# High parts cast on ScalarE, block 0's weights copied on GpSimd, and the first clip ahead of the first additions

## What is computed

```python
d2 = q2[..., :, None] + k2[..., None, :] - 2.0 * qk
W = jnp.power(EPS + jnp.sqrt(jnp.maximum(d2, 0.0)), -2)
W = W / (EPS + jnp.sum(W, axis=-1, keepdims=True))
H = G * jnp.einsum('hbts,hbse->hbte', W, V)
```

## Time and profile before

| | before |
|---|---|
| median of three runs | 1596.91 us |
| the profiled execution | 1595.71 us |
| its span, first to last instruction | 1593.9 us |
| TensorE busy | 1420.5 us |
| VectorE busy | 1032.5 us |
| ScalarE busy | 928.3 us |
| GpSimd busy | 650.6 us |
| TensorE's mean granted clock | 0.962 |

### The profile page before, as it was taken

One profiled execution on the slowest core, in us unless ns is written; L12 is line 12 of the kernel. 1 busy time (PEld: TensorE's weight loads), 2 busy tenths in 40 slices (PEclk: granted clock), 3 DMA queues, 4 the chain that ended last, 5 costly groups with the idle time before them and its releaser, 6 DMA issues. The chain is left out here.

```text
span 1593.9 us, 23093 instructions
## 1 busy us (share of the span) xinstructions
PE 1420.5 (89%) x7425; PEld 902.2 (57%) x7426; DVE 1032.5 (65%) x1359; ACT 928.3 (58%) x646; POOL 650.6 (41%) x484
## 2 busy tenths in 40 slices
PE   6899999999999999999997568888983799999996
PEld 4555555555555555555454257777773566666664
DVE  7878988898889888988887635555566321221221
ACT  1779888988898889888989412222221122222221
POOL 5255456545654565456532612122120233333331
PEclk9999999999999999999999779999995899999998
DMA  4000000000000000000000312111120034233312
GB/s 144 14 1 14 27 26 13 13 26 26 13 13 26 26 13 13 26 27 13 7 13 14 112 57 97 39 52 40 46 81 13 21 85 138 33 84 84 87 28 71
DMA packets 67484, 66.91 MB, mean 42 GB/s; under 512 B 5152, under 2 KB 59936, under 8 KB 67424
## 3 DMA queue, kind: packets, MB, share of 16 engines
q1 hardware_dynamic: 60160, 56.58, 10.9%
q0 software_dynamic: 7296, 9.97, 3.7%
HBM read 48.70 MB, written 19.92 MB: 43 GB/s over the span
## 5 line engine op out<-in xcount | busy, mean ns | idle before, releaser
L1612 POOL TENSOR_TENSOR v_aug<-v_aug,wts 128x1024 f32<-128x1024 f32 x96 | 254.4, 2650 | 249.2 <-ACT wts L1465 244.6
L983 DVE TENSOR_SCALAR wts<-ps_s,k 128x1024 f32<-128x1024 f32 x240 | 297.1, 1279 | 86.3 <-PE ps_s L537 66.0
L1457 ACT ACTIVATE wts<-wts 128x4096 f32<-128x4096 f32 (+1 forms) x80 | 231.8, 2935 | 88.0 <-DVE wts L983 66.8
L552 PE MATMUL ps_o<-wts,g_r 128*64 128x512 f32 x1024 | 252.6, 616 | 12.7 <-ACT wts L1465 12.5
L1463 ACT ACTIVATE wts<-wts,eps_d 128x4096 f32<-128x4096 f32 (+1 forms) x80 | 241.6, 3019 | 0.2
L1465 ACT ACTIVATE wts<-wts 128x4096 f32<-128x4096 f32 (+1 forms) x80 | 235.2, 2940 | 2.5
L1378 DVE TENSOR_TENSOR wts<-rinv,ps_s 128x352 f32<-128x352 f32 x76 | 39.6, 521 | 254.5 <-ACT rinv L1530 171.3
L778 PE MATMUL ps_s<-wts,qk 128*128 x608 | 198.6, 470 | 3.2 <-issue 2.3
L972 DVE TENSOR_TENSOR v_aug<-v_aug,wts 128x1024 f32<-128x1024 f32 x96 | 156.1, 1626 | 5.4 <-ACT wts L1465 5.1
L537 PE MATMUL ps_s<-q_hi,k_hi 64*128 64x512 f32 x512 | 115.8, 446 | 41.2 <-DVE wts L983 31.1
L778 PEld LDWEIGHTS ps_s<-wts,qk 128*128 128x128 f32 x608 | 110.8, 192 | 65.2 <-issue 17.5
(11 more groups left out here) (238 smaller groups left out, 2411.7 us busy)
## 6 DMA issues: line engine op xcount, KB each, us to landing
wts<-in_w SPq DMA_DIRECT2D x16, 704.0 KB, 5.5
h_t<-o_raw SPq DMA_DIRECT2D x16, 512.0 KB, 2.7
qk<-h_t SPq DMA_DIRECT2D x16, 512.0 KB, 4.0
wts<-in_w SPq DMA_DIRECT2D x8, 640.0 KB, 7.1
raw_qk<-in_w_in SPq DMA_DIRECT2D x32, 128.0 KB, 2.2
raw_vg<-in_w_in SPq DMA_DIRECT2D x32, 128.0 KB, 2.2
acc<-wts SPq DMA_DIRECT2D x17, 128.0 KB, 1.8
wts<-in_x SPq DMA_DIRECT2D x2, 1024.0 KB, 5.9
```

The costliest lines, as they stand in the source:

```text
L552: mm = pe.matmul(ps_o[r, t], v_pair[:, b, r], wts[:, h, b, t], start=b == 0, stop=b == SB - 1)
L983: dve.tensor_scalar(wts[:, h, b, :], ps_s[:, h, :], k2[:, 2 * b + h:2 * b + h + 1], 0.0, ALU.add, ALU.max).then_inc(S_.max_ok, 1)
L1457: act.activation(chunk(start, end), chunk(start, end), ACT.Sqrt).then_inc(S_.sqrt_ok, 1)
L1612: pool.tensor_tensor(acc_w[:, 0], acc_w[:, 0], wts[:, 0, b], ALU.add).then_inc(S_.add_ok, 1)
```

## The change

It has four parts.

- The casts of q and k to their high parts move from VectorE's tail to ScalarE, between its square roots of blocks 6 and 7. They wait for q and k of the pair, and for the distances of the pair before, which still read the old high parts.
- A new semaphore, `acc0_ok`, and a new function `copy_first` on GpSimd, at the start of its body: it waits for block 0's weights and for the row sums of the pair before, and copies block 0 of both heads into `acc_w`, as a product with a column of ones.
- `add_first` then adds only block 1, into `acc_w` in place. `guard` of block 0 waits for the copies, that of block 1 for the additions, as before.
- On VectorE, `add_first` moves behind the guard of block 0 (in the last body, which has no guards, it stays where it was).

```diff
--- before.py
+++ after.py
@@ -247,7 +247,7 @@
         tok_i = sb("tok_i", [P, ET], U32)
         tok_now = sb("tok_now", [P, 2], U32)
 
-        names = ("x_in", "xb_in", "cst_in", "c_in", "fill_s", "fill_ok", "xnb_ok", "stats_ok", "aggr_ok", "std_ok", "rstd_ok", "xn_ok", "tr_ok", "xnt_ok",
+        names = ("x_in", "xb_in", "cst_in", "c_in", "fill_s", "fill_ok", "xnb_ok", "acc0_ok", "stats_ok", "aggr_ok", "std_ok", "rstd_ok", "xn_ok", "tr_ok", "xnt_ok",
                  "qk_in", "vg_in", "wqk_ok", "wvg_ok", "xh_ok", "x2_in", "q_proj", "k_proj", "v_proj", "g_proj", "norm_mm", "k2_mm",
                  "v_turned", "s_ready", "av_blk", "sum_mm", "q_ok", "k_cp", "vt_ok", "g_ok", "hi_ok", "split_ok", "qn1", "qn_ok", "k2_ok",
                  "v_ok", "max_ok", "h_ok", "sqq_ok", "sqk_ok", "add0_ok", "add_ok", "addb_ok", "gr_ok", "sqrt_ok", "ln_ok", "w_ok", "rln_ok", "r_ok", "h_out",
@@ -958,10 +958,9 @@
 
             def add_first(n):
                 dve.wait_ge(S_.w_ok, len(LOGS) * n + parts_until(LOGS, 1))
-                if not (isinstance(n, int) and n == 0):
-                    dve.wait_ge(S_.sum_mm, n)
                 for h in range(2):
-                    dve.tensor_tensor(acc_w[:, h], wts[:, h, 0], wts[:, h, 1], ALU.add).then_inc(S_.add0_ok, 1)
+                    dve.wait_ge(S_.acc0_ok, 2 * n + h + 1)
+                    dve.tensor_tensor(acc_w[:, h], acc_w[:, h], wts[:, h, 1], ALU.add).then_inc(S_.add0_ok, 1)
 
             def add_second(n, b):
                 dve.wait_ge(S_.w_ok, len(LOGS) * n + parts_until(LOGS, b))
@@ -972,8 +971,8 @@
                 dve.tensor_tensor(acc_w[:, 1], acc_w[:, 1], wts[:, 1, b], ALU.add).then_inc(S_.addb_ok, 1)
 
             def guard(n, b, free):
-                if not (isinstance(n, int) and n == 0) and b <= 1:
-                    dve.wait_ge(S_.add0_ok, 2 * n)
+                if b <= 1:
+                    dve.wait_ge((S_.acc0_ok, S_.add0_ok)[b], 2 * n)
                 if free is not None:
                     dve.wait_ge(S_.addb_ok, free)
                 dve.wait_ge(S_.s_ready, SB * (n - 1) + b + 1)
@@ -1023,8 +1022,8 @@
 
                 if ahead >= 1:
                     dve.wait_ge(S_.k2_ok, p + 2)
-                add_first(p)
                 if ahead == 0:
+                    add_first(p)
                     context()
                 for b in range(SB):
                     if b == 6 and not first:
@@ -1037,9 +1036,9 @@
                         add_second(p, b)
                     if ahead >= 1:
                         guard(p + 1, b, NA * p + (b - 1) if b >= 2 else None)
+                    if b == 0 and ahead >= 1:
+                        add_first(p)
                 copy_values(p)
-                if ahead == 2:
-                    split_high(p + 2)
                 if ahead >= 1:
                     copy_vt(p + 1, p + 3 if ahead == 2 else PAIRS)
                 if ahead == 2:
@@ -1448,9 +1447,18 @@
                 act.wait_ge(S_.rln_ok, n + 1)
                 act.activation(rinv[:], rinv[:], ACT.Exp, scale=-1.0).then_inc(S_.r_ok, 1)
 
-            def roots(n):
+            def split_high(n):
+                act.wait_ge(S_.q_ok, n + 1)
+                act.wait_ge(S_.s_ready, SB * (n - 1))
+                act.activation(q_hi[:], q32[:], ACT.Copy)
+                act.wait_ge(S_.k_cp, n + 1)
+                act.activation(k_hi[:], k32[:], ACT.Copy).then_inc(S_.hi_ok, 1)
+
+            def roots(n, ahead=False):
                 for start, end in ROOTS:
-                    if isinstance(n, int) and start in (2, 4):
+                    if ahead and end == SB:
+                        split_high(n + 1)
+                    if isinstance(n, int) and n == 0 and start in (2, 4):
                         turned_high(start + 2)
                         turned_high(start + 3)
                     act.wait_ge(S_.max_ok, NB * n + 2 * end)
@@ -1468,9 +1476,11 @@
 
             roots(0)
             weights(0, True)
-            with act.Fori(1, PAIRS) as p:
-                roots(p)
+            with act.Fori(1, PAIRS - 1) as p:
+                roots(p, ahead=True)
                 weights(p, False)
+            roots(PAIRS - 1)
+            weights(PAIRS - 1, False)
             rows(PAIRS - 1)
 
             def probs_t(i, k, n):
@@ -1603,6 +1613,13 @@
                     pool.wait_ge(S_.k2_mm, n)
                 pool.tensor_tensor(k_sq[:], k32[:], k32[:], ALU.mult).then_inc(S_.sqk_ok, 1)
 
+            def copy_first(n):
+                pool.wait_ge(S_.w_ok, len(LOGS) * n + parts_until(LOGS, 0))
+                if not (isinstance(n, int) and n == 0):
+                    pool.wait_ge(S_.sum_mm, n)
+                for h in range(2):
+                    pool.tensor_tensor(acc_w[:, h], wts[:, h, 0], unit, ALU.mult).then_inc(S_.acc0_ok, 1)
+
             def add_block(n, b):
                 pool.wait_ge(S_.w_ok, len(LOGS) * n + parts_until(LOGS, b))
                 if b == 2:
@@ -1619,6 +1636,7 @@
 
             def pair(p, first=False, ahead=2, later=3):
 
+                copy_first(p)
                 for b in range(2, SB):
                     if b == 4 and not first:
                         gate_rows(p - 1)
```

## The result

The changed kernel took 1658.45 us in the median of four runs (1657.16 to 1661.7), the kernel before 1596.62 in four: a ratio of 1.0392, with a 95% interval of 1.0374 to 1.041. The forecast was 1652 us.

The account below looks back on a forecast made before the run. Bound: a loop over the engines where ScalarE's weights and VectorE's tail meet at block 2's values, 53.0 us a pair. 14 x 4.1 = 57, less 1 for the last, 56; 1595.7 + 56 = 1652 us, range 1606 to 1662.

Parts of the forecast that it names:

- Step 1: ScalarE's hole before its last square root: the two moved casts, 2.1 us, fit with 0.3 us or more to spare.
- both strands: ScalarE's weights and VectorE's tail of copies, then guards, meeting at block 2's values on TensorE, each with under 0.2 us spare.
- the lock: Shared port pair: VectorE operations with two SBUF inputs and GpSimd operations wait for each other whole, taking turns.
- Steps 2 and 3: VectorE's tail comes 1.21 us earlier, low part of q asked at 338.75; GpSimd's copies, 1.93 us each, ask at 338.57.
- the rival in which VectorE gets in first: VectorE's low part of q runs before GpSimd's first copy: 0.4 to 1.25 us a pair, 1601 to 1613 us, chance 0.18.
- Step 4: VectorE's low parts take turns with GpSimd's copies; k2 copy at 344.65, TensorE at 345.2, 2.4 us later.
- Step 5: Block 0's guard ahead of the first additions wins 0.3 us at most; guard at 347.4, block 2's values 2.3 us later.
- the first collision: VectorE's low parts against GpSimd's copies of block 0's weights: +2.3 us a pair.
- Steps 6 and 7: Block 2's guard 2.4 us later; then VectorE's block 4 addition collides with GpSimd's of block 6: one pair costs +4.1 us.
- Only the first collision counts: Rival: later phases of the loop close up without the second collision; +2.3 us a pair, 1628 us, chance 0.17.
- faster: Rival: GpSimd's copy doesn't take the lock, low parts stay at 1.21 us; 1587 to 1596 us, chance 0.06.
- ScalarE is not in the way: Rival denied here: ScalarE's casts end after 331.1 or load a table; 1 us late gives 14, within the last 0.04.

Follow-up runs that it names:

- experiment 7: Changed kernel plus ten unused matmuls in TensorE's wait before block 0's distances: 1653.51 us, beside 1659.32 us for the changed kernel on the same chip.
- experiment 6: Changed kernel plus three waits on GpSimd (additions of blocks 3 and 6, square of q) that let VectorE go first: 1627.16 us, ratio 1.0195.
- experiment 3: Changed kernel without its move: casts on ScalarE, copies on GpSimd, block 1's additions ahead of block 0's guard again: 1631.93 us, ratio 1.0214.
- experiment 2: Changed kernel with casts back on VectorE and `add_first` in its old place, so only GpSimd's copies remain: 1631.27 us, ratio 1.0204.
- experiment 1: Kernel before with only the two casts moved to ScalarE: 1588.99 us, ratio 0.9952.

## Why the prediction was right, and where it wasn't

**Step 1, the casts at no cost: right.** They take 1.06 and 1.04 us, and the last root waits for its guard, idle for 1.19 us in front of it. **That a gain in VectorE's tail is worth 0.2 us at most: wrong.** The casts alone gave 0.42 a pair. TensorE's start of block 2's values, for which both strands counted, moved by 0.15. But I had counted only as proof of the lock, and not as 3.44 us inside the circle that 0.1 us of lead would shorten. In the whole change this gain is lost again, as block 2's addition takes 3.12 us there.

**Steps 2 and 3: right in mechanism and nearly in size.** Laid over the rows of before, the turned values start at 332.99 (I had 332.79), the copies ask at 338.48 (338.57), the low part of q at 338.97 (338.75). The margin I worried about was 0.5 us, not 0.18: the rival in which VectorE gets in first had less behind it than the 0.18 I gave it.

**Step 4: right, 0.4 us too large.** The k2 copy begins at 344.2 (344.65) and TensorE starts at 344.7, 2.0 us late instead of 2.4. Taking turns is as forecast. **Step 5 made that good by another error**: I kept 2.06 us for the distances, and with the lower clock they took 2.6, so the guard starts at 347.4, exactly as forecast. The clock stood nowhere in the prediction. It put in 0.5 us where the first collision lacked 0.4. That the two cancel is luck, and of this pair: over 13 passes the distances and the wait behind them range from 2.15 to 3.72 us (experiment 7).

**Steps 6 and 7: right to 0.3 us, with one collision left out.** The guard of block 2 starts at 358.2 (358.2), that of block 4 at 370.0 (370.05), the addition of block 5 asks at 372.4 (372.4) and the guard behind it starts at 375.1 (375.45). But block 3's addition is held up as well, 2.98 us behind GpSimd's of block 4 (380.57 and 380.07). No step has that. Little of it reaches block 4, as its guard and the copy of q behind it had 1.1 and 0.7 us to spare before. The idle time of about 1 us that I had in front of block 5's distances is there (1.06); the one in front of block 6's is not.

The 4.1 us a pair came out as 57.1 - 53.0 = 4.1, but not the split. I had 2.3 for the first collision and 1.8 for what follows. At full clock, the kernel with the first collision and without the later ones but block 3's has 54.2 us, 1.6 above the casts alone (52.56), where block 2 has its turn too; the later ones add 2.6. Against the kernel before, the casts' gain of 0.4 goes off and the lower clock puts 0.3 on: 1.6 + 2.6 - 0.4 + 0.3 = 4.1. The mechanism is the forecast one, but that the total is right to the tenth is in part luck.

**The count of pairs was short by one.** Thirteen periods and the end give 53.4 + 2.6 = 56.0, but the agreement with the forecast's 56 is by chance, as the first of the fourteen tails lies ahead of the first k2 copy. The prologue makes low parts beside GpSimd's copies too:

```profile
72.33 2.56 DVE L925 TENSOR_TENSOR q_lo<-qk,q_hi 128x1024 fp32r<-128x1024 f32 x1
74.81 2.91 DVE L926 TENSOR_TENSOR k_lo<-norms,k_hi 128x1024 fp32r<-128x1024 f32 x1
...
122.06 1.22 DVE L957 COPY o_raw<-ps_o 128x1024 f32<-128x1024 f32 x1
```

The first body's value copy, at 122.06, stood at 119.01 before. So of the 5.3 us ahead of the first k2 copy, 3.1 come from this fifteenth collision and the first body, which I hadn't counted, and 2.2 are the first of the fourteen. The fourteen cost 2.2 + 53.4 + 2.6 = 58.2 us, where I had 56. The fifteenth is more than half of the difference between 1652 and the 1657.16 us of the profiled execution.

**The rivals.** "Only the first collision counts" falls with experiment 6; "faster" falls with the low parts' 2.48 and 2.91 us. ScalarE is not in the way: with the copies, the kernels with and without its casts have the same periods at full clock. The share of the move (1.5 us a pair, experiment 3; 1.8 at full clock) was in the sum, through step 6, but I never priced the move by itself, and so missed that it loses.

VectorE gave no work to GpSimd here: its additions are as many as before, and the 28 casts went to ScalarE. The Trainium skill's warning on moving work between VectorE and GpSimd (Perfetto Trace Analysis, "Optimizing Scalar/DVE Operations") gives their shared read port as its reason. The traces agree that work on GpSimd isn't free for VectorE: the copies alone cost 35 us (experiment 2).

## What to carry to other kernels

Where VectorE works with two SBUF inputs (or casts from SBUF, see below), a GpSimd operation in this kernel costs the wait that it imposes on VectorE, and not its own time. Look at when the two ask, and for durations above the shortest of a line, as such a wait shows as busy time and names no releaser. A loop in which both add into the same tile is a row of turns; in the changed kernel three waits on GpSimd that let VectorE go first gave 2.2 us a pair (experiment 6), the casts taken off VectorE 0.4 (experiment 1). Count the prologue and the first body when a cost per pass is multiplied. And when a total comes out right, check its terms one by one: here two were off and cancelled.

## What the runs showed of the hardware that I hadn't expected

- The lower clock came behind a short idle time in a loop that is otherwise full: 2.76 us of TensorE idle, then granted clocks of 0.76 and 0.81 over the next 8 us. It didn't come behind every such gap: in 4 of 13 passes the distances stayed at full clock. With the idle time filled the clock stayed at 1.00 (experiment 7), and in the kernel before, whose gap there is 0.64 us, it is 1.00 over 80 to 880 us too. The Trainium skill (TensorE: Matmul & The Clock Gate, "What's actually happening") names idle time as what takes the engine back to the lower level; the traces agree in kind.
- A lag of a few hundredths decides 2.2 us of one operation. Before, VectorE's addition of block 2 asked 0.04 us behind GpSimd's and lost; with the casts gone it asked 0.2 us ahead and took 1.27 us.
- Two inputs in SBUF aren't needed. In the prologue of the kernel before, a cast of one SBUF tensor on VectorE takes 2.42 us, asked 0.02 us behind a GpSimd square. The cast of k in the loop, with no GpSimd operation beside it, takes 0.68. So the casts that moved to ScalarE had waited too: the first of them takes 1.23 us in the earlier trace rows, beside a GpSimd split that ends at 332.93.

```profile
63.77 1.90 POOL L1604 TENSOR_TENSOR k_sq<-norms 128x1024 f32<-128x1024 f32 x1 [13.23 <-DVE norms L914]
63.79 2.42 DVE L920 CAST q_hi<-qk 128x1024 fp32r<-128x1024 f32 x1
...
333.40 0.68 DVE L921 CAST k_hi<-norms 128x1024 fp32r<-128x1024 f32 x1
331.50 1.43 POOL L1585 TENSOR_TENSOR wqk_lo<-raw_qk,wqk_hi 128x256 fp32r<-128x256 f32 x2
```
